# r in high and low parts in every FFN step, the first norm on ACT and POOL, output sums in place

## The reference

```python
# attention block
a  = layernorm(x)
q, k, v = a @ Wq + bq, (a @ Wk + bk) @ Wc @ We, (a @ Wv + bv) @ Wc @ We
# 16 heads of 16, 4 key/value heads, feature map elu(.) + 1, causal linear attention
o  = sum_{s<=t} (qf_t . kf_s) v_s / (sum_{s<=t} qf_t . kf_s + 1e-6)
y  = a + o @ Wo + bo
x2 = x + layernorm(y) * gamma + beta
# FFN block
z  = layernorm(x2);  zprev = z shifted by one token
xr, xk = mu_r * z + (1 - mu_r) * zprev, mu_k * z + (1 - mu_k) * zprev
out = x2 + sigmoid(xr @ W_r) * (square(relu(xk @ W_k)) @ W_v)
```

## Time and profile before

| what | value |
|---|---|
| median of 3 runs | 272.54 us (272.11 to 272.74) |
| the profiled execution | 272.06 us |
| its span, first to last instruction | 270.3 us |
| PE, PE weight load | 258.1 us (95%), 195.4 us (72%) |
| DVE | 233.2 us (86%) |
| ACT | 168.8 us (62%) |
| POOL | 149.0 us (55%) |
| granted TensorE clock | 1.000, the upper level, throughout |

### The profile page before, as it was taken

The page is one execution under the profiler, slowest core; times in us unless marked ns, Lnnn a source line. Parts: engine busy times, 40 slices in busy tenths (PEclk is TensorE's granted clock), DMA queues, the critical chain, the costliest instruction groups (busy, mean ns, idle before and its releaser), DMA issues.

```text
span 270.3 us, 7775 instructions
## 1 busy us (share of the span) xinstructions
PE 258.1 (95%) x3047; PEld 195.4 (72%) x3047; DVE 233.2 (86%) x562; ACT 168.8 (62%) x339; POOL 149.0 (55%) x171
## 2 busy tenths in 40 slices
PE   7998989999998999999999999999999999999893
PEld 6867657877874788759875888758875877686663
DVE  6677779889799899998999899996999868999694
ACT  2579786794667856586648765686348730357570
POOL 3567484579944695366833685366433533173542
PEclk9999999999999999999999999999999999999999
DMA  6910320000200040002200020002000020000213
GB/s 180 266 67 4 79 80 2 4 2 0 81 2 0 2 158 0 2 4 76 82 2 0 2 81 1 2 4 78 2 0 4 2 80 2 0 0 0 80 42 116
DMA packets 12180, 10.75 MB, mean 40 GB/s; under 512 B 2288, under 2 KB 12144, under 8 KB 12144
## 3 DMA queue, kind: packets, MB, share of 16 engines
q1 hardware_dynamic: 11392, 9.97, 12.1%
q10 hardware_dynamic: 752, 0.30, 0.5%
HBM read 6.07 MB, written 4.19 MB: 38 GB/s over the span
## 4 chain that ended last, share of the span: by engine, by line
PE 52%; DVE 26%; ACT 9%; issue 6%; POOL 4%; DMA 2%; ACTq 0%; DVEq 0%; POOLq 0%
PE ps_x L539 7%; PE ps_x L524 7%; PE ps_x L546 5%; PE ps_z L495 5%; PE ps_x L428 4%; PE ps_x L577 4%; PE ps_y L511 4%; PE ps_y L516 4%; DVE xk L1201 4%; DVE stats L1068 3%; DVE probs L1142 3%; DVE qf L1106 2%; DVE xr L1201 2%; PE ps_x L532 2%; ACT eq L848 2%
## 5 line engine op out<-in xcount | busy, mean ns | idle before, releaser
L1142 DVE TENSOR_TENSOR probs<-ps_z,causal 128x1024 f32<-128x1024 f32 x32 | 38.7, 1209 | 2.6 <-PE ps_z L495 2.3
L276 POOL TENSOR_TENSOR xb_tok<-x_in,beta_bc 128x1024 f32<-128x1024 f32 x8 | 19.1, 2382 | 21.0 <-DVE x_tok L1186 21.0
L524 PE MATMUL ps_x<-wo_sb,oT 128*128 128x256 f32 x128 | 30.1, 383 | 0.0
L284 POOL TENSOR_TENSOR prod<-qf,ksum 128x1024 f32<-128x1024 f32 x7 | 16.6, 2365 | 24.1 <-DVE ksum L1115 24.1
L299 POOL TENSOR_TENSOR out_tok<-tanh_r,x_tok 128x512 f32<-128x512 f32 x14 | 18.3, 1314 | 19.6 <-DVE tanh_r L1213 19.3
L524 PEld LDWEIGHTS ps_x<-wo_sb,oT 128*128 128x128 f32 x128 | 23.4, 190 | 3.8 <-issue 0.5
L269 POOL TENSOR_TENSOR abo_tok<-a_tok,bo_bc 128x1024 f32<-128x1024 f32 x8 | 18.9, 2368 | 11.9 <-DVE kf L1100 3.5
L495 PE MATMUL ps_z<-qf,kfT 32*128 32x128 f32 x512 | 23.3, 296 | 1.6 <-ACT kfT L828 1.3
L229 POOL TENSOR_TENSOR rstd<-rstd,neg_half 128x4 f32<-128x4 f32 x22 | 23.0, 1046 | 1.7
L495 PEld LDWEIGHTS ps_z<-qf,kfT 32*128 32x128 f32 x512 | 17.2, 185 | 7.3 <-issue 3.6
L511 PE MATMUL ps_y<-qf,state 32*32 32x128 f32 x512 | 20.5, 274 | 1.0 <-DVE oT L1154 0.4
(11 more groups left out here) (194 smaller groups left out, 683.2 us busy)
## 6 DMA issues: line engine op xcount, KB each, us to landing
x_in<-in_L_attn_x_dram SPq DMA_DIRECT2D x8, 512.0 KB, 4.6
out_dram<-out_tok SPq DMA_DIRECT2D x16, 256.0 KB, 2.1
xr<-in_L_attn_Wq_dram ACTq DMA_DIRECT2D x1, 256.0 KB, 4.1
xk<-in_L_ffn_W_r_dram SPq DMA_DIRECT2D x1, 256.0 KB, 5.0
xk<-in_L_ffn_W_k_dram SPq DMA_DIRECT2D x1, 256.0 KB, 5.2
xr<-in_L_ffn_W_v_dram SPq DMA_DIRECT2D x1, 256.0 KB, 5.8
wo_sb<-in_L_attn_Wo_dram SPq DMA_DIRECT2D x4, 64.0 KB, 4.6
bo_bc<-in_L_attn_bo_dram SPq DMA_DIRECT2D x1, 128.0 KB, 5.0
```

The lines of the kernel that those rows point to most:

```text
L276: PL.tensor_tensor(xb_tok[n % 2][:], x_in[n % XBUF][:], beta_bc[:].unsqueeze(1).to_broadcast([P, NB, D]), ALU.add).then_inc(s_xb, 1)
L524: last = mm(bk_[:, (b % 2) * D:(b % 2 + 1) * D], oT[m % 2][:, a, b, :], wo_sb[:, a, :], start=(a == 0), stop=(a == 1))
L1142: V.tensor_tensor(probs[b % 2][:].rearrange("p g (r s) -> p g r s", s=HALF), ps_z[:, :, 0:2 * P].rearrange("p g (r s) -> p g r s", s=HALF) ...
```

## The change

It has four parts. (1) `mix_r` in steps 2 to 6 becomes `mix_r_parts`: ACT copies xr into a high part (`high_xr`), DVE makes the low part (`low_xr`), TensorE sums three products (24 matmuls a step). The parts get tiles of their own. (2) The first norm of y in these steps goes the way of step 1: POOL also makes a bias (`scale_and_bias`), ACT normalises y in four instructions, POOL multiplies by gamma and adds `xb_tok` in eight; DVE's `centre` and `second_residual` go. (3) `finish` writes the output sum into `x2_tok` instead of `out_tok`, and the stores read it there; waits for stores move accordingly. (4) `prod` lies in the queries' tile `eq`. The finale keeps its plain `mix_r` and DVE's way of the first norm.

```diff
@@ -90,7 +90,7 @@
         ksum = pair("ksum", NB, P)
-        prod = sb("prod", 2, T)
+        prod = eq
         rden, rden_bc = sb("rden", P), pair("rden_bc", NB, 2, P)
@@ -104,7 +104,8 @@
         wr_p = [ctx.enter_context(nc.sbuf_tensor(f"wr_{part}", [P, KD, D], F32R)) for part in ("high", "low")]
-        xr_p, wr_split, s_xrh, s_xrl = aT_p, sem("wr_split"), sem("xr_high"), sem("xr_low")
+        xr_p = [ctx.enter_context(nc.sbuf_tensor(f"xr_{part}", [P, KD, T], F32R)) for part in ("high", "low")]
+        wr_split, s_xrh, s_xrl = sem("wr_split"), sem("xr_high"), sem("xr_low")
         s_aTh, s_aTl, wq_split = sem("aT_high"), sem("aT_low"), sem("wq_split")
@@ -114,7 +115,7 @@
         xk, xr = sb("xk", KD, NB, P), sb("xr", KD, NB, P)
-        k_act, tanh_r, out_tok = sb("k_act", 2, T), sb("tanh_r", 2, 512), sb("out_tok", NB, D)
+        k_act, tanh_r = sb("k_act", 2, T), sb("tanh_r", 2, 512)
@@ -170,6 +171,7 @@
         ka_value = lambda m: 2 * m + 2 if m < LAST - 1 else 2 * m
+        xr_value = lambda m: 2 * m + 2 if m < LAST else 2 * (LAST - 2) + 2
         x_value = lambda n: 16 * (n // XBUF) + 16
@@ -188,8 +190,10 @@
                         sp.wait_ge(s_lastp, i + 1)
+                    if m >= 1:
+                        sp.wait_ge(out_stored[i], 16 * m)
                     sp.dma_start(chunk_at(out, m)[:, 2 * i:2 * i + 2, :],
-                                 out_tok[:, 2 * i:2 * i + 2, :]).then_inc(out_stored[i], 16)
+                                 x2_tok[m % 3][:, 2 * i:2 * i + 2, :]).then_inc(out_stored[i], 16)
@@ -248,12 +252,16 @@
             def scale_residual(m):
+                if m >= 3:
+                    for i in range(2):
+                        pool.wait_ge(out_stored[i], 16 * (m - 2))
+                    pool.wait_ge(s_z, 4 * m - 8)
                 for b in range(NB + 1):
                     if b < NB:
-                        pool.wait_ge(s_n1, b + 1)
+                        pool.wait_ge(s_n1, 4 * m + b + 1)
                         PL.tensor_tensor(y_tok[:, b, :], y_tok[:, b, :], gamma_bc[:], ALU.mult).then_inc(s_t, 1)
                     if b:
-                        pool.wait_ge(s_t, b)
+                        pool.wait_ge(s_t, 4 * m + b)
                         PL.tensor_tensor(x2_tok[m % 3][:, b - 1, :], y_tok[:, b - 1, :], xb_tok[m % 2][:, b - 1, :],
@@ -294,9 +302,7 @@
                     pool.wait_ge(s_gt, 2 * m + i + 1)
-                    if m >= 1:
-                        pool.wait_ge(out_stored[i], 16 * m)
-                    PL.tensor_tensor(out_tok[:, 2 * i:2 * i + 2, :], tanh_r[:, i].rearrange("p (b d) -> p b d", b=2),
+                    PL.tensor_tensor(x2_tok[m % 3][:, 2 * i:2 * i + 2, :], tanh_r[:, i].rearrange("p (b d) -> p b d", b=2),
                                      x2_tok[m % 3][:, 2 * i:2 * i + 2, :], ALU.add).then_inc(s_out, 1)
@@ -307,7 +313,8 @@
                     add_bo(n)
-                    first_norm(m)
+                    scale_and_bias(m, mv1, neg_mean1, rstd1, nbias1, s_st1, s_rs1, s_nb1)
+                    scale_residual(m)
                     add_beta(n)
@@ -356,8 +363,7 @@
                     pool.wait_ge(s_gl, 2 * i + 1)
-                    pool.wait_ge(out_stored[i], 16 * c)
-                    PL.tensor_tensor(out_tok[:, 2 * i, :], tanh_r[:, i, 0:D], x2_tok[c % 3][:, 2 * i, :],
+                    PL.tensor_tensor(x2_tok[c % 3][:, 2 * i, :], tanh_r[:, i, 0:D], x2_tok[c % 3][:, 2 * i, :],
                                      ALU.add).then_inc(s_lastp, 1)
@@ -547,15 +553,15 @@
-            def mix_r_parts(i, bk_):
-                pe.wait_ge(s_xrh, 2)
+            def mix_r_parts(m, i, bk_):
+                pe.wait_ge(s_xrh, xr_value(m))
                 for b in (2 * i, 2 * i + 1):
...
                     if b == 0:
-                        pe.wait_ge(s_xrl, 2)
+                        pe.wait_ge(s_xrl, xr_value(m))
                     for k in range(KD):
@@ -658,9 +664,10 @@
                     pe.wait_ge(s_y, 2 * m + (1 if f else 2))
-                    mix_r(f, 0, x1)
+                    pe.wait_ge(wr_split, 2)
+                    mix_r_parts(f, 0, x1)
                     pe.wait_ge(s_y, 2 * m + 2)
-                    mix_r(f, 1, x2)
+                    mix_r_parts(f, 1, x2)
                 outputs(c, 0)
@@ -762,9 +769,9 @@
                 pe.wait_ge(wr_split, 2)
-                mix_r_parts(0, z2)
+                mix_r_parts(c, 0, z2)
                 pe.wait_ge(s_th, 2 * m + 2)
-                mix_r_parts(1, z3)
+                mix_r_parts(c, 1, z3)
                 pe.wait_ge(s_gt, 2 * m + 1)
@@ -845,6 +852,7 @@
                     act.wait_ge(s_qf, 2 * n - 1 + a)
+                    act.wait_ge(s_den_ps, n)
                 AC.activation(eq[:, a, :], bk_[:, :], ACT.Relu, bias=neg_bq[:, a:a + 1], scale=-1.0).then_inc(s_nq, 1)
@@ -929,6 +937,13 @@
                     copy(ka_p[0][:, n, :], k_act[:, n, :]).then_inc(s_kah, 1)
+
+            def high_xr(m):
+                if m >= 1:
+                    act.wait_ge(s_r_ps, 2 * m)
+                for k in range(KD):
+                    act.wait_ge(s_xr, 2 * m + k + 1)
+                    copy(xr_p[0][:, k, :], xr[:, k].rearrange("p b t -> p (b t)")).then_inc(s_xrh, 1)
@@ -952,6 +967,8 @@
                     reciprocals(c)
+                if f >= 0:
+                    high_xr(f)
                 for k in range(KD):
@@ -973,6 +990,7 @@
                     gate_r(f, 1, x2)
+                    normalise_y(m)
                 queries(n, 0, x0)
@@ -1010,9 +1028,7 @@
                 gate_r(m, 1, z3)
-                for k in range(KD):
-                    act.wait_ge(s_xr, 2 * c + k + 1)
-                    copy(xr_p[0][:, k, :], xr[:, k].rearrange("p b t -> p (b t)")).then_inc(s_xrh, 1)
+                high_xr(c)
                 channel_k(c, 0, z0, True)
@@ -1179,8 +1195,8 @@
                 if m >= 3:
-                    dve.wait_ge(s_out, 2 * m - 4)
-                    dve.wait_ge(s_z, 4 * m - 8)
+                    dve.wait_ge(out_stored[0], 16 * (m - 2))
+                    dve.wait_ge(out_stored[1], 16 * (m - 2))
                 for b in rows:
@@ -1228,17 +1244,14 @@
                 token_shift(f, 1, *for_r)
-                if f == 0:
-                    add_residual(m, 1, x1)
                 if f >= 1:
                     add_residual(m, 0, x1)
-                    add_residual(m, 1, x2)
+                low_xr(f)
+                add_residual(m, 1, x2 if f else x1)
                 mask(c, 1)
                 keys_values(n)
-                centre(m)
                 key_features(n)
                 low_a(n)
-                second_residual(m)
                 divide(c, 0)
@@ -1262,6 +1275,14 @@
                     V.tensor_tensor(aT_p[1][:, k, :], aT[:, k, :], aT_p[0][:, k, :].bitcast(F32), ALU.subtract).then_inc(s_aTl, 1)
+
+            def low_xr(m):
+                if m >= 1:
+                    dve.wait_ge(s_r_ps, 2 * m)
+                for k in range(KD):
+                    dve.wait_ge(s_xrh, xr_value(m) - 1 + k)
+                    V.tensor_tensor(xr_p[1][:, k, :], xr[:, k].rearrange("p b t -> p (b t)"), xr_p[0][:, k, :].bitcast(F32),
+                                    ALU.subtract).then_inc(s_xrl, 1)
@@ -1342,10 +1363,7 @@
                 token_shift(c, 1, *for_r)
-                for k in range(KD):
-                    dve.wait_ge(s_xrh, k + 1)
-                    V.tensor_tensor(xr_p[1][:, k, :], xr[:, k].rearrange("p b t -> p (b t)"), xr_p[0][:, k, :].bitcast(F32),
-                                    ALU.subtract).then_inc(s_xrl, 1)
+                low_xr(c)
                 gate(m, 0, x1)
@@ -1357,9 +1375,8 @@
                     if b % 2:
-                        dve.wait_ge(out_stored[i], 16 * c)
                         dve.wait_ge(s_gl, b + 1)
-                        V.tensor_tensor(out_tok[:, b, :], tanh_r[:, i, cols], x2_tok[c % 3][:, b, :], ALU.add).then_inc(s_last, 1)
+                        V.tensor_tensor(x2_tok[c % 3][:, b, :], tanh_r[:, i, cols], x2_tok[c % 3][:, b, :], ALU.add).then_inc(s_last, 1)
```

## The result

The changed kernel takes 275.07 us (median of 4 runs, 275.01 to 275.14), the kernel before on the same chip 272.4: ratio 1.0097 [1.0085, 1.011]. The prediction of 275.2 was right in time and sign. Its largest term, for steps 3 to 6, was 1.1 us too high, and 0.95 us that it did not have or had too small came in elsewhere: the total is close in part by luck.

A forecast was written before the change was run, and what follows sets the result against it. TensorE's instruction stream was taken as the bound, with a side chain to `mix_k` without slack. Steps 3 to 6 (+2.4) and step 2 (+0.45) gave +2.85 us on 272.06: 274.9, or 275.4 by the runs' median; predicted 275.2, range 270.6 to 277.8.

The forecast's parts named there:

- largest term: Steps 3 to 6: DVE and POOL block each other, +0.6 us a step, +2.4 us in all.
- The side chain: From the queries' first half to `mix_k`: no slack; blocked `xk` lengthen TensorE's step by 0.55 us, bounds -0.5 and +0.9.
- four passes for fp32: r on TensorE: three products cost three quarters of plain fp32, saving 0.89 us a step; not the figure taken.
- The pair of `xk`: DVE, amid POOL's eight instructions: the two `xk` wait 1.05 us together, bounds 0 and 1.4.
- The lock read from the finale: DVE and POOL alternate, each waiting out the other's whole instruction; finale's `xk` lasts 1.52 us, 0.70 unhindered.
- POOL's path: POOL's eight instructions, `xb_tok`, then `prod`: `prod` ends at 180.6, TensorE wants it at 180.55; +0.6 us a step.
- The missed term: Step 2 was predicted at +0.45 us, bounds -1.4 and +1.2, and the finale at 0.
- r's wait of 0.83 us: Step 2: low parts stand before y's second half, so TensorE waits 0.85 us before r.
- Slack of 0.2 us: ACT in step 5: norm of y ends at 170.45, queries' first half at about 170.65.
- The rival with a late norm: Much slower: late nbias1 holds `eq` back 0.5 us, `xk` waits 1.4 us; 278.5 us, chance 0.12.
- Side edits at nothing: Output sums in place, reuse of `x2_tok` and `prod` in `eq`: their waits are hidden and cost nothing.
- The faster one: No blocking where it counts: each step keeps its 0.5 us, 2.0 to 2.5 us less, 270.1 us; chance 0.2.

The follow-up runs named there:

- both moves: The changed kernel with DVE's two `xk` moved before `divide(c, 0)` and POOL's `add_beta` put behind `second_norm`; 269.42 us, ratio 0.989.
- the second move: POOL's `add_beta` put behind `denominator_terms` and `second_norm`; alone on the changed kernel it measured 274.37 us, ratio 1.0077.
- POOL's fills: The kernel before with ten POOL memsets into a spare tile added in front of `add_beta` in steps 2 to 6; 273.1 us, ratio 1.0033.
- the kernel with the low parts after y: The kernel with both moves, and in step 2 the low parts of xr behind the second half of y on DVE; 272.72 us, ratio 1.0025.
- the kernel with the added reads: The kernel before with eight POOL products into a spare tile added in front of `add_beta` in steps 2 to 6; 282.17 us, ratio 1.0357.

## Why the prediction was right, step by step

**The total.** Close in part by luck. Against the span of before, steps 3 to 6 cost 1.30 us where 2.4 were predicted, 1.1 too much. Step 2 cost 0.43 more than predicted, the finale 0.33 and the start 0.19, 0.95 too little.

**What bounds the kernel.** Right. The side chain over `eq`, `qf` and the two `xk` had no slack, and it is the chain after. Taking the pair off it, and `add_beta` out of the product's way, turned +2.7 us into -3.1.

**r.** The saving was predicted at 0.5 us a step from `mix_v_parts` and measures 0.58 (3.45 to 2.87). The other figure that the prediction weighed, four passes for fp32 by the Trainium skill (FP8 and Floating Point Precision, TensorE Precision Notes), gives 0.89; the trace does not agree: 0.83 of the old time, not three quarters. With all waits away the steps confirm it: 30.13 us with plain r and both moves, 29.51 with three products, 0.62 apart.

**The pair of `xk`.** Predicted +1.05 us (0 to 1.4), measured +0.93, with both instructions stretched and both residual sums beside them. The lock read from the finale was the right mechanism. Its price for one meeting was too high: the first `xk` met a POOL instruction that had started only 0.08 us before, so by the prediction's working, where each waits out the other's whole 0.70, the pair would have lost 1.3 us. It lost 0.93, some 0.47 for each instruction, and the mean of 0.35 that the prediction took for the first one made up most of the difference.

**The mis-sized term: +0.6 a step.** The side chain alone gave the prediction +0.55, then POOL's path +0.6, and the larger was taken. The side chain gave +0.34. Of the 0.26 too much, 0.20 are two sizes (0.08 of r, 0.12 of the pair), and the rest is POOL's path: I had the eight instructions begin at 169.05 and end at 175.9, and the product 0.05 us late. In the step the product ends 0.15 us early. I had POOL lose 1.3 us to the pair, but the eight take 6.48 us for the 5.58 of the earlier trace rows, which is 0.90. So the product comes 0.3 us earlier in the step than I had it, and TensorE, late itself by the same pair, asks for it only 0.1 earlier. Steps 3 to 6 cost 1.30 us, not 2.4.

**The missed term: step 2, and 0.33 us of the finale.** r's wait of 0.83 us was right to 0.02. `mix_k`, +0.24 from the step's start, was also below the +0.45. Missing was POOL's product: the prediction looked at this queue in step 5 only, where it fits by 0.15 us, and not in step 2, where it does not (0.60 us idle, where the row of before above has none). The step cost 0.88. That `add_beta` moved alone brings 0.7 us shows it. The finale's growth is one late instruction at its end. The chains of the kernel before and of the changed one:

```profile
266.73 0.04 issue
266.77 0.43 DVE tanh_r L1357
```

```profile
269.13 0.40 issue
269.52 0.43 DVE tanh_r L1375
```

TensorE's last matmul starts 40.07 us after the last `scores` before and 40.11 after the change; the last gate on DVE behind it then starts 0.36 us later, and waits for nothing that the profile shows. All five kernels here that have both parts of the change show 0.40 or 0.41 there (from the last `scores` to the end of the span 44.4 to 44.5 us), the other seven 0.04 (44.1 to 44.2). So neither part alone causes it; what does stays open. The 0.19 us ahead of step 2 is the spread of the start, and no part of the change.

**ACT.** Slack of 0.2 us before `eq` was predicted and 0.20 measured. The rival with a late norm did not happen, though nbias did take 0.59 us instead of 0.20, as feared.

**Side edits at nothing.** Right (0.9998 [0.9989, 1.0007]).

**The rivals.** The faster one named its own condition, that the side chain and POOL's chain lose under 0.5 us a step together; they lose 0.93 at one place. It is not wrong about the size of the gain, only about the place of `xk`: its 2.0 to 2.5 us are what the two moves got, and 0.6 more.

## What to carry to other kernels

When work moves from VectorE to GpSimd, compare not only lengths but places: list the VectorE instructions whose inputs are all in SBUF, see which fall inside the new GpSimd stretch and lie on the chain that ends last, and move those away. A blocked instruction shows no wait in the profile, only a greater length, so compare each with the shortest of its group. A queue that fits in one step must be shown to fit in the odd steps too, and behind a limit that is removed the next one must be looked for: here the second move was worth 4.1 us behind the first, and 0.7 alone.

## What the runs showed of the hardware that I had not expected

POOL's fills hinder DVE not at all (1.67 and 1.40 us, to the hundredth what they are alone), while reads of the same length more than double the residual (3.60 for 1.67 us).

The length of a block follows what is left of the instruction that is met, and is 0.1 to 0.2 us shorter in the three cases that the rows above allow to be worked out. The first `xk` of the changed kernel finds 0.64 us left of a 128x256 product and lasts 1.19 us, where one alone takes 0.75; the second finds 0.66 left and lasts 1.22; the first `xr_low` in step 2 of the kernel with the low parts after y finds 2.01 us left of a 128x1024 sum, and the two take 3.16 us for 1.28. Long GpSimd instructions are the dangerous neighbours.

In the kernel with the added reads the granted clock fell in step 2. The stage window there:

```profile
85.00:92.50 7.50, 7.04 (x38) 3.38 (x36) 6.44 (x18) 2.99 (x8) 6.78 (x6) 0.62 0.00 0
```

And its timeline of PE:

```profile
82.45 0.64 PE L517 MATMUL ps_y<-qf,state 32*32 32x128 f32 x16 [1.66 <-DVE oT L1160]
...
86.69 5.67 PE L545 MATMUL ps_x<-xk,wkT 128*128 128x512 f32 x8 [0.46 <-DVE qf L1112]
```

After idle stretches of 1.66 and 0.46 us the mean granted clock of this window is 0.62 (the levels are 1.2 and 2.4 GHz, 1.00 is the upper), and `mix_k` takes 5.67 us for 3.70. The kernel with the low parts after y, whose idle in step 2 is 3.25 us, has 1.00 there in its profiled execution, but not over all its runs: six at a mean clock of 0.999 or 1.000 took 271.91 to 272.31 us, four at 0.993 or 0.994 took 273.12 to 273.40, and two at 0.987 took 274.83 and 274.84. The kernel with the added reads varies too: two executions at a mean clock of 0.998 and 1.000 took 281.02 and 281.44 us, two at 0.988, the profiled one among them, 282.90 and 282.94. So beside its own length a wait can come with a lower clock in some executions, for 1.7 us in one kernel and up to 2.7 in the other. No trace was kept of an execution of the second kernel at the lower clock, so that its clock falls at the 3.25 us is not shown, and what decides in which executions it falls stays open. In step 5 all twelve kernels have 1.00, the one with the reads too, whose TensorE waits 0.28 and 1.25 us in it.
